# Bringing a residual back from DRAM in runs of three tokens before the last addition

## The reference

```python
h = tok(x, W, b)                          # overlapping patches -> (64, 93, 128)
h = h + attn(layernorm(h), ...)           # 8 heads, causal, ALiBi, projections with 3-tap convolutions
h = h + ffn(layernorm(h), ...)

def ffn(hidden, gate_weight, w1, w2):     # 16 experts, top 2
    h = silu(einsum('td,efd->tef', x, w1))
    h_mean = einsum('tef,te->ef', h, mask) / max(counts, 1)   # one mean per expert
    y_mean = einsum('ef,edf->ed', h_mean, w2)                 # 16 rows of 128
    return einsum('tk,tkd->td', routing_w, y_mean[top_idx])
```

## Time and profile before

| | us |
|---|---|
| median of 3 runs (744.2 to 747.3) | 744.61 |
| the profiled execution | 743.62 |
| its span, first to last instruction | 742.0 |
| mean granted clock of TensorE | 0.986 |
| first addition of the end (L1400) starts | 727.43 |
| last addition (L1400) starts | 738.40 |

### The profile page before, as it was taken

How to read it: one execution, slowest core, us unless ns; L and a number is a source line. 1 busy time by engine, 2 the same in 40 slices (tenths; PEclk the granted TensorE clock), 3 DMA queues, 4 the chain that set the end, 5 groups by cost and what they waited for, 6 DMA issues and landing times.

```text
span 742.0 us, 21226 instructions
## 1 busy us (share of the span) xinstructions
PE 698.6 (94%) x6576; PEld 625.0 (84%) x6576; DVE 573.8 (77%) x1596; ACT 603.0 (81%) x2014; POOL 378.2 (51%) x392
## 2 busy tenths in 40 slices
PE   7889999999999999999999999998888897999996
PEld 7868898888898888989898989886676687999994
DVE  5177677888778888778788878888888779888876
ACT  4558998989898989999898989787786786899860
POOL 5742434676556566666666665645362556222200
PEclk9999999999999999999999999999999999999997
DMA  8131124232222121221212222102135113122206
GB/s 312 57 85 42 52 91 152 74 120 54 68 61 52 52 57 49 55 52 52 76 52 55 53 73 54 34 12 73 28 79 192 28 50 84 51 65 65 64 19 166
DMA packets 44274, 54.01 MB, mean 73 GB/s; under 512 B 13651, under 2 KB 31251, under 8 KB 43696
## 3 DMA queue, kind: packets, MB, share of 16 engines
q1 hardware_dynamic: 30048, 38.84, 18.1%
q0 software_dynamic: 12544, 12.87, 6.5%
q10 hardware_dynamic: 1616, 1.48, 0.6%
HBM read 42.69 MB, written 10.26 MB: 71 GB/s over the span
## 4 chain that ended last, share of the span: by engine, by line
PE 42%; DVE 29%; ACT 19%; issue 7%; DMA 1%; DVEq 1%; POOL 0%; ACTq 0%
ACT prob L909 11%; DVE qkv L1101 6%; PE psTP L506 5%; DVE qkv L1104 5%; PE psSO L788 5%; PE psTP L508 4%; PE psTP L507 4%; PE psTP L788 4%; DVE prob L1242 4%; PE psSO L655 3%; PE psSO L600 3%; DVE rmin L1193 3%; ACT qkv L878 3%; PE psSO L636 3%; PE psSO L617 2%
## 5 line engine op out<-in xcount | busy, mean ns | idle before, releaser
L1492 POOL DMA_INDIRECT expert_rows<-hn,slot x128 | 168.0, 1312 | 52.4 <-issue 32.1
L909 ACT ACTIVATE prob<-psSO,rmin 93x93 f32<-93x93 f32 x512 | 151.6, 354 | 8.8 <-DVE rmin L1193 7.9
L1410 POOL TENSOR_TENSOR x_lo<-x_raw,x_hi 128x752 fp32r<-128x752 f32 x58 | 104.8, 1808 | 46.3 <-ACT x_hi L870 45.8
L1101 DVE SCALAR_TENSOR_TENSOR qkv<-psTP,taps,qkv 128x368 f32<-128x368 f32 x192 | 112.7, 587 | 18.9 <-ACT qkv L878 17.1
L1104 DVE SCALAR_TENSOR_TENSOR qkv<-psTP,taps,qkv 128x364 f32<-128x364 f32 x192 | 114.4, 596 | 6.8
L878 ACT ACTIVATE qkv<-psTP,taps 128x372 f32<-128x372 f32 x192 | 112.8, 588 | 8.0 <-PE psTP L508 7.5
L909 ACT ACTIVATION_READ_ACCUMULATOR prob<-psSO,rmin 93x1 f32 x512 | 98.0, 191 | 0.0
L506 PE MATMUL psTP<-x_hi,wtok_hi 128*128 128x376 f32 x232 | 88.1, 380 | 0.0
L506 PE MATMUL psTP<-xnT_hi,wqkv_hi 128*128 128x372 f32 x192 | 77.2, 402 | 8.1 <-DVE qkv L1104 7.6
L1166 DVE TENSOR_REDUCE part<-qkv 128x4 f32<-128x512 f32 (+1 forms) x108 | 72.2, 679 | 8.2 <-ACT qkv L926 3.7
L508 PE MATMUL psTP<-x_hi,wtok_lo 128*128 128x376 f32 x232 | 77.8, 335 | 0.0
(11 more groups left out here) (215 smaller groups left out, 1745.0 us busy)
## 6 DMA issues: line engine op xcount, KB each, us to landing
x_raw<-in_x SPq DMA_DIRECT2D x58, 376.0 KB
w1s<-in_w POOLq DMA_DIRECT2D x8, 512.0 KB
w<-in_w SPq DMA_DIRECT2D x4, 1024.0 KB
out<-resid SPq DMA_DIRECT2D x16, 160.0 KB, 2.7
xsE<-expert_rows SPq DMA_DIRECT2D x36, 64.0 KB, 1.8
xs<-expert_rows SPq DMA_DIRECT2D x36, 64.0 KB, 1.8
xs<-expert_rows POOLq DMA_DIRECT2D x36, 64.0 KB, 2.1
x_first_raw<-in_x SPq DMA_DIRECT2D x6, 376.0 KB, 7.1
```

What stands on the lines that cost most here:

```text
L909: i = nc.scalar.activation(prob[:, a, hh, :], psS[:NT, a, hh * NT:(hh + 1) * NT], ACT.Exp, bias=rmin[:, a, hh:hh + 1], scale=-1.0, accum_o ...
L1101: nc.vector.scalar_tensor_tensor(dst[:, :, 1:NT], src[:, :, 0:NT - 1], taps[:, k, 1:2], dst[:, :, 1:NT], ALU.mult, ALU.add).then_inc(tap1_ ...
L1410: nc.gpsimd.tensor_tensor(lo[:, 0:PIECE], src, hi[:, 0:PIECE].bitcast(F32), ALU.subtract)\
L1492: nc.gpsimd.indirect_dma_start(rows, bass.IndirectOffsetOnAxis(slot[1 - u][:, c:c + 1], 0), hn[1 - u][:, c % GB, :], None)\
```

## The change

Of `resid` only the way to the last addition changes. SP writes it out to a DRAM tensor `parked` in the order of the output, one DMA per 16 sequences (`park`): three of the four where the loads of `x` have ended, ahead of the first part of `fetch_early`, the fourth ahead of `tails`. Before its last round of 12 tiles ACT issues the way back (`unpark`): one DMA for every fourth sequence, 16 sequences each, which puts three consecutive tokens of a sequence on a partition. `resid3` has sequence b of a group on the 31 partitions from 32b on, 384 values (1,536 bytes) per group. Two more DMAs fill the partitions 95 and 127 with other values of `parked`.

The products follow: for each group twelve in place of four, each for every third token of one sequence, with 32 columns in place of 93, and all of a group in one bank of 128 x 384. `NO` goes from 2 to 8. An addition covers 128 x 384 in place of 93 x 512 and waits, before the first, for all that `unpark` brings. `store` issues one DMA for one sequence position of two groups: 31 partitions x 2 x 1,536 bytes; SP has positions 0 and 1, ACT 2 and 3, 16 DMAs each.

```diff
     rows = nc.dram_tensor("expert_rows", [ROWS, D], F32, kind="Internal").ap()
+    parked = nc.dram_tensor("parked", [B, NT, D], F32, kind="Internal").ap()
     ctx = ExitStack()
     with ctx:
         def sb(name, shape, dt=F32):
...
         mean = sb("mean", [128, FB, E * ESTRIDE])
-        rwT = sb("rwT", [128, NG * NT])
+        rwT = sb("rwT", [128, NG * NT + 3])
         vrow = [sb(f"vrow{u}", [NT, H, DH]) for u in range(2)]
         hn = [sb(f"hn{u}", [NT, GB, D]) for u in range(2)]
         hnT = sb("hnT", [D, GT])
...
         tokT = sb("tokT", [D, GT])
-        resid = sb("resid", [NT, B * D])
+        resid_all = sb("resid", [128, B * D])
+        resid = resid_all[:NT, :]
+        RUN = 3
+        PARTS = NT // RUN
+        resid3 = resid_all[:, 0:NG * RUN * D].rearrange("p (g c) -> p g c", g=NG)
         stat = sb("stat", [NT, GB, 6])
         mv = sb("mv", [NT, GB, 2])
         veps = sb("veps", [NT, GB])
...
         tab_e = sb("tab_e", [1, 2 * 128], I32)
-        NR, NX, NO = 6, 4, 2
+        NR, NX, NO = 6, 4, 8
         DOWN_COLS = 128 // ESTRIDE
-        OUT_ROWS = ((0, 80), (80, NT))
         AHEAD = 3
         late = [qkv[u][:].rearrange("p k b n -> p (k b n)") for u in range(2)]
...
         psS, psO = psSO[:, 0:2, :], psSO[:, 2:4, :]
-        psMix = [psTP, psSO]
         psWout = psO[:NT, 0, 384:512]
         psLate = psP[1][:NT, 384:512]
         psTot = psO[:, 1, 0:E]
...
-        psOut = [psX4[:NT, :, :] for psX4 in psMix]
+        psOut = [ps4[:, k, 0:RUN * D] for ps4 in (psTP, psSO) for k in range(4)]
         psX = [psS[:, 0, :], psS[:, 1, :], psV, psTok]
...
         mean_zero, mix_mm, out_add = sem("mean_zero"), sem("mix_mm"), sem("out_add")
+        parked_out, parked_in = sem("parked_out"), sem("parked_in")
         out_done = [sem(f"out_done{p}") for p in range(2)]
         ACT_PIECES = {(0, 0): (2, 3), (0, 1): (4,), (0, 2): (5,), (0, 3): (6,), (1, 0): (7,), (1, 1): (), (1, 2): ()}
...
-        def run_tiles(eng, body):
+        def run_tiles(eng, body, last=None):
             for k in range(ROUND):
                 body(EARLY // ROUND, k)
             with eng.Fori(EARLY // ROUND + 1, NTILE // ROUND - 1) as r:
                 for k in range(ROUND):
                     body(r, k)
+            if last:
+                last()
             for k in range(ROUND):
                 body(NTILE // ROUND - 1, k)
...
-            lo, hi = OUT_ROWS[part]
-            for g in range(NG):
-                eng.wait_ge(out_add, g + 1)
-                eng.dma_start(out[g * GB:(g + 1) * GB, lo:hi, :].rearrange("b t d -> t b d"),
-                              resid[lo:hi, g * GB * D:(g + 1) * GB * D].rearrange("t (b d) -> t b d", d=D))\
-                    .then_inc(out_done[part], 16)
+            for g in range(0, NG, 2):
+                eng.wait_ge(out_add, g + 2)
+                for b in (2 * part, 2 * part + 1):
+                    eng.dma_start(by_runs(out, b)[:, g:g + 2, :],
+                                  resid3[b * ESTRIDE:b * ESTRIDE + PARTS, g:g + 2, :]).then_inc(out_done[part], 16)
             eng.wait_ge(out_done[part], 16 * NG)
+
+        def by_runs(dram, b):
+
+            return dram.rearrange("(g b) (p r) d -> b p g (r d)", b=GB, r=RUN)[b]
+
+        def park(eng, g):
+
+            eng.wait_ge(res_add, (g + GB) * GB)
+            eng.dma_start(parked[g * GB:(g + GB) * GB, :, :].rearrange("n t d -> t n d"),
+                          resid[:, g * GB * D:(g + GB) * GB * D].rearrange("t (n d) -> t n d", d=D))\
+                .then_inc(parked_out, 16)
+
+        def unpark(eng):
+
+            eng.wait_ge(parked_out, 16 * (NG // GB))
+            for b in range(GB):
+                eng.dma_start(resid3[b * ESTRIDE:b * ESTRIDE + PARTS, :, :], by_runs(parked, b)).then_inc(parked_in, 16)
+            filler = parked.rearrange("n t d -> (n t d)")[0:NG * RUN * D].rearrange("(o c) -> o c", o=1)
+            for p in (3 * ESTRIDE - 1, 4 * ESTRIDE - 1):
+                eng.dma_start(resid_all[p:p + 1, 0:NG * RUN * D], filler).then_inc(parked_in, 16)
         block = ctx.enter_context(nc.Block())
...
             sp.dma_start(rows[E * CAP:ROWS, :], zeros[:, :]).then_inc(zero_tile_out, 16)
+            for g in range(0, NG - GB, GB):
+                park(sp, g)
             fetch_early(sp, 0, NRE)
             sp.wait_ge(proj_mm, NG * NBLK)
             for j in range(1, FB):
                 sp.dma_start(w2s[j][:, :, :], w2[:, j, :, :]).then_inc(late_w_in, 16)
             fetch_early(sp, NRE, EARLY - NRE)
+            park(sp, NG - GB)
             sp.wait_ge(tail_ready, 1)
             tails(sp)
             fetch_tiles(sp, 0)
...
             pe.wait_ge(ymix_ready, 1)
+            pe.wait_ge(rwzero_ready, 2)
             def mix(g, u):
                 wait(pe, out_add, g - (NO - 1))
-                for b in range(GB):
-                    mm = nc.tensor.matmul(psOut[u][:, b, 0:D], rwT[b * ESTRIDE:(b + 1) * ESTRIDE, g * NT:(g + 1) * NT],
-                                          ymix[b * ESTRIDE:(b + 1) * ESTRIDE, :], start=True, stop=True)
+                for r in range(RUN):
+                    for b in range(GB):
+                        rows_b = slice(b * ESTRIDE, (b + 1) * ESTRIDE)
+                        mm = nc.tensor.matmul(psOut[u][rows_b, r * D:(r + 1) * D],
+                                              rwT[rows_b, g * NT + r:g * NT + r + ESTRIDE * RUN - RUN + 1:RUN],
+                                              ymix[rows_b, :], start=True, stop=True)
                 mm.then_inc(mix_mm, 1)
             for g in range(NG):
...
             silu_quad(LAST_QUADS[-1], 3, 1)
-            run_tiles(ac, tile)
+            run_tiles(ac, tile, lambda: unpark(ac))
             store(ac, 1)
...
             run(dve, step)
+            nc.vector.memset(rwT[:, NG * NT:], 0.0).then_inc(rwzero_ready, 1)
             steps = [0]
...
+            dve.wait_ge(parked_in, 16 * (GB + 2))
             for g in range(NG):
                 dve.wait_ge(mix_mm, g + 1)
-                res = resid[:, g * GB * D:(g + 1) * GB * D]
-                res = res.rearrange("t (b d) -> t b d", d=D)
-                nc.vector.tensor_tensor(res, psOut[g % NO][:, :, 0:D], res, ALU.add).then_inc(out_add, 1)
+                nc.vector.tensor_tensor(resid3[:, g, :], psOut[g % NO], resid3[:, g, :], ALU.add).then_inc(out_add, 1)
         @block.gpsimd
```

## The result

The change makes the kernel 31% slower: 979.63 us median (978.02 to 980.48, 4 runs) against 744.73 us, a ratio of 1.3149 with a 95% interval of 1.3125 to 1.3174. The forecast was 992 us, with a range of 944 to 1034. The profiled execution took 978.02 us.

What follows compares the result with a forecast made beforehand. PE, busy 94% of 742.0 us, was taken to bound the kernel, additions its last stage. First addition 855.1, two additions 1.1, DMA overhead 2.2 and stores 132 make 990.4; with 1.6 more, 992 us, range 944 to 1034.

Steps and rivals of the forecast that it cites:

- One engine for 31 partitions: Way back and stores: a DMA over 31 partitions, a prime, gets one DMA engine; 132 us each way.
- the rival that 31 x 16 count together: Both dimensions set the engines: way back 8 us and hidden, stores 66 us, 798 us in all; chance 0.04.
- The sum: Whole kernel: 855.1 + 1.1 + 2.2 + 132 = 990.4 us of span, 992 us with 1.6 between span and time.
- The packet: Way back and stores: a packet of 1,536 bytes costs an engine 66.5 ns, with bounds of 58 and 93.
- the rate of the 8,192-byte rows: Lower bound for the packet price: 312 ns per 8,192 bytes, 26.3 GB/s, which makes 58 ns for 1,536 bytes.
- ACT held: Issuing the way back blocks ACT, and the last 12 tiles behind it, until 832.3, 125.1 us late; chance 0.53.
- one row of 2.05 us: Issue of `w_out` in the earlier profile, taken as a full queue holding the issuer; other issues cost about 0.4.
- First addition: Start of the last stage: 727.4 + 125.1 = 852.5, plus 2.6 for the clock, so 855.1 us.
- the clock: PE's first products after idling for 120 us run slowly: 2.6 us added ahead of the first addition.
- The fourth park: Way out after 605.7, ahead of the zeros: 13.8 us on three engines, cost taken as 0, bound 1 us.
- The first three parks: Way out behind L489: 13.8 us each on three engines, done at about 544, covered by 32 us, cost 0.
- Products and additions: Last stage: first eight groups' products ready before the wait ends, an addition some 0.55 us, both far ahead of the stores.

Runs made afterwards that it cites:

- experiments 1 to 3: Changed kernel with stores split over 16 and 15 partitions (876.52 us), with the way back over 32 partitions (865.74 us), and with both edits (759.23 us).
- experiment 7: Kernel before the change, each group's store as one DMA over all 93 partitions in place of 80 and 13: 781.65 us, ratio 1.0489.
- experiment 4: Changed kernel with stores over 16 and 15 partitions, way back over 32, and parks split into 80 and 13: 755.05 us, ratio 1.0129.
- Experiment 3: Changed kernel with stores over 16 and 15 partitions and way back over 32, parks still over 93: 759.23 us, ratio 1.0195.

## Why the prediction was right

**One engine for 31 partitions:** right, shown by experiments 1 to 3 for 31 and by experiment 7 for 93. Of the rival that 31 x 16 count together nothing is left: the way back had 6.5% of sixteen engines, and the rival's count was all sixteen. The sum puts all DMAs over 31 partitions on the same engine; no row of before shows that. The runs do: q1 and q10 have 3.3% each and 25 GB/s together from 860 to 970 us, what q10 alone had on the way back (24 GB/s).

**The packet.** Forecast 66.5 ns, measured 62 to 63.5: a DMA of 496 packets takes 31.0 us on ACT, and the 1,984 of the stores went in 123 us against 132. I had drawn a line through two rows; the rate of the 8,192-byte rows, 58 ns, was as near. This price is the term that was mis-sized: the span was 14.0 us below my 990.4, of which the hold is 5.4 and the stage from the first addition to the end 9.4 (125.9 for 135.3), less 0.8 in the other terms.

**ACT held.** Right, on the evidence of one row of 2.05 us, so with some luck; I had given it 0.53. Forecast 125.1, measured 119.7 us. The sum frees ACT when all but 130 packets are through; no run shows that limit. What the runs show is near in number and other in form: the issues end at 709.56, 735.20, 766.21 and so on. At 735.20 some 381 of the first DMA's 496 packets had gone, at 766.21 some 877 in all, and so on. So here an issue ends when some 115 packets of the DMA before it are left, with the whole of the DMA just issued behind them.

**First addition.** Forecast 855.1, measured 850.50: ACT reached the way back 1.8 later than at 707.24, was held 5.4 less, and from its first copy (828.83) to the addition went 21.7 us, 1.5 above the 20.2 of before, where I had put 2.6 for the clock. The 1.8 too little and the 1.1 too much nearly cancel, which is luck.

**The fourth park,** taken as 0 with a bound of 1 us, was the one term whose bound failed. SP's timeline of the changed kernel:

```profile
501.86 29.35 SPq L465 DMA_DIRECT2D parked<-resid  x3
532.33 37.18 SPq L395 DMA_DIRECT2D xsE<-expert_rows  x24
...
613.63 24.59 SPq L447 DMA_DIRECT2D expert_rows<-zeros  x16
640.24 69.44 SPq L378 DMA_DIRECT2D xs<-expert_rows  x36
```

The first three parks were free as forecast: PE turned the first early tile at 590.83, within 0.5 us of before. Behind the fourth the zeros took 24.59, not 17.44, and the fetches began at 640.24, 7.5 us late and 4 later than my bound allowed. SP wasn't held ahead of the zeros, as I had assumed, but in them: with the park over 80 and 13 partitions they take 18.35 us (experiment 4). That the zeros' own shares queued on the three engines behind the park fits this and is argued. In this kernel it cost ACT 1.8 us on its way to the last round. Experiment 3 reaches that point 3.0 us later than experiment 4 (709.85 against 706.86) and the first addition 4.7 later.

**Products and additions** were not a term of the sum, rightly: four additions take 2.45 us, all sixteen 10.3. That eight groups' products would be ready when the wait ends was wrong, though. With ACT held PE's products come late too, they start at 849.49, and the first addition waits for PE (1.06 us in its row).

## What to carry over

Read the partition counts of a DMA before anything else: on SP's and ACT's queues 31 partitions got one engine (pieces of 1,536 bytes) and 93 three (pieces of 512 and 2,976), and splitting 31 into 16 and 15, or padding to 32, gave 103 and 114 us back for a leg of 3 MB. Then ask which partitions are filled at one time: the same pieces went at 203 GB/s into 32 and at 382 GB/s into 128. Then ask what stands behind the transfer in time: issued ahead of the last tiles' fetches and spread over sixteen engines, the way back still made one of them land after 8.9 us in place of some 2. Larger pieces bought nothing here. DVE's additions filled the last stage before, and each further DMA costs its engine 0.4 to 1.6 us of issue behind the last addition.

## What the runs showed of the chip that I had not expected

- On one DMA engine, the issue of a further DMA holds the issuing engine until some 115 packets of the DMA before it are left, 31.0 us a piece at 496 packets, and with it all compute instructions behind it.
- POOL's queue cut a DMA of 31 partitions into packets of 4,608 and 12 bytes, at 41 GB/s and the time of 2.8 engines.
- Sixteen engines into 32 partitions take 127 ns for a packet of 1,536 bytes that one engine alone does in 62, with the share of the DMA engines at over 100%: busy engines are no sign of a full rate.
- The kernel's first 500 us, to which no variant adds an instruction, end (SP's issue of `w`) between 500.7 and 505.7 us in the profiled executions, so versions within 1% of each other can't be ranked by one profile.
